# Edge counts of a graph kernel stored as bytes, cast by ScalarE, with other sizes of transfer and another schedule of the matrix writes

## Chip, core and metric

One core of a Trainium2 chip runs the whole program in one launch. The metric is device time in microseconds. The kernel before took 3538.95 us, the median of three runs (3537.87 to 3542.65).

## What is computed

The reference is a block of two graph networks on 6250 nodes of 256 features, with 100000 edges that come sorted by destination. First an attention layer, then three SAGE layers, each on the normalised activations and added to them. Cut to what matters here:

```python
h = relu(layernorm(x))
x = x + attention(h, edge_attr_16, edge_attr_4, ..., src, dst)
h = relu(layernorm(x))
for l in range(3):
    msg = relu(h @ pW[l] + pb[l])[src]
    agg = segment_sum(msg, dst)
    mean = agg / maximum(deg, 1)
    out = mean @ lW[l] + lb[l] + h @ rW[l]
    h = out / norm(out)              # silu after layers 0 and 1
x = x + layernorm(h) * ln_w + ln_b
```

## The kernel before, in words

Nodes are tiled into 49 blocks of 128 (`BLOCKS`), edges into 782 tiles of 128, seven tiles to a chunk of the attention (`CHUNKS` = 112). The program is three phases with a barrier between them: `prepare` (node projections), `attention`, and `layers` (three sweeps, one per SAGE layer). Every engine runs its own list of instructions in order, written out by hand; semaphores order them against each other.

**The two ways in which messages are summed.** For destinations from column 2008 on (`FIRST_TILE` = 251), POOL gathers the message rows of the source nodes by indirect DMA, 128 rows at a time (line 1174, 531 gathers in each sweep), and PE sums them with small one-hot matrices (line 1310). For the first 2048 destinations (`DENSE`) the sum is a dense product instead: a matrix of edge counts, 6272 sources by 2048 destinations, is built in DRAM once (`m.adj`, fp32) and streamed in each sweep. A step of the dense product (`sweep_step`, lines 1233 to 1242) takes one block of 128 sources and 512 destination columns: two fp32 matmuls of 128x128 by 128x512 (line 1240). There are 4 passes by 49 blocks = 196 steps in a sweep. `stream` on SP (lines 1179 to 1186) loads for each step a 128x512 piece of the matrix (line 1184) and the 128x256 message block (line 1186) into one of six buffers (`STREAM`), and waits for PE to free it.

**How the matrix is built, inside the attention phase.** DVE finds for each of the first 261x128 edges how many edges of the same cell stand before and after it (`count_piece`, lines 587 to 612): 18 pieces, one in every second chunk from chunk 2 on (`COUNT_FROM`), then `place_cells` makes the cell's address and count. SP clears the matrix with 49 stores, one per chunk from chunk 1 (`ZERO_FROM`, line 1673). POOL then writes the counts by indirect DMA, 128 cells at a time (`place_edges`, line 580), 261 writes in all: from chunk 60 on (`BUILD_FROM`), evenly over the chunks, with 44 left (`LATE_CELLS`) until after the last chunk's gathers.

**The order in the attention.** POOL gathers the seven tiles of chunk c (line 571) once chunk c - 7 is summed (`RING` = 7 buffers, the wait on `summed`), and in the same list come the matrix writes. The other engines run a pipeline over several chunks: PE projects and transposes scores of later chunks while it sums earlier ones (line 1743, and line 1751, which ends a chunk and releases its buffer). `layers` begins when POOL has seen all its writes land (`built`) and the other engines have drained.

**The order in a sweep.** It has 67 chunks of up to eight edge tiles. In chunk q, PE sums the gathered tiles (line 1310), then does the dense steps that `steps_done(q)` gives, three or four of them, and within them the work on one node block: `combine` (line 1278), `project` (line 1288). ACT in chunk q runs `keep` (line 1472, the gathered sums out of PSUM), then for a node block `first` (lines 1481, 1485) and `second` (square at line 1493, Silu at line 1496), and after each of the four passes `turn` (line 1515, two copies of 128x512). SP in chunk q sends the loads for the steps up to `steps_done(q - 1)` + 6 and then stores finished message blocks (line 1207). POOL gathers up to ten groups of tiles ahead (`QUADS`), and waits for `summed`.

Of the kernel before, what the change touches and what calls it, by code (L numbers as in the profile page):

```python
# [30 lines left out]
int32 = mybir.dt.int32  # L31
ALU = mybir.AluOpType
# [3 lines left out]
P = 128  # L36
N, E, D = 6250, 100000, 256
HEADS, HD, KINDS, FEATS = 8, 32, 4, 16
LAYERS = 3
# [48 lines left out]
COUNT_FROM = 2  # L88
COUNT_ROOT = 32
ZEROS = 1024  # L90
# [7 lines left out]
ZERO_FROM, BUILD_FROM, LATE_CELLS = 1, 60, 44  # L98
# [1038 lines left out]

def layers(nc, m, a):
# [5 lines left out]
                            stream0=None, stream1=None, stream2=None, stream3=None, stream4=None, stream5=None,  # L1144
                            streamed=STREAM, turned=1,
# [18 lines left out]
    with stack:  # L1164
# [13 lines left out]
        def _(sp):  # L1178
            def stream(w, d):

                u = w.step0 + d
                k, j, part = u % STREAM, d % BLOCKS, d // BLOCKS
                sp.wait_ge(s["streamed"].sem, s["streamed"].free(u))
                sp.dma_start(m.a_rows[:, k, 0:PASS_COLS[part]],
                             m.adj[j * P:(j + 1) * P, PASS_AT[part]:PASS_AT[part] + PASS_COLS[part]]).then_inc(s[f"stream{k}"], 16)
                sp.dma_start(m.m_rows[:, k, :], block_rows(m.tables[w.l], j)).then_inc(s[f"stream{k}"], 16)
# [22 lines left out]
            sp.dma_start(m.dst_at, m.at_dram).then_inc(s["places"], 16)  # L1209
            for w in sweeps:  # L1210
# [21 lines left out]
        def _(pe):  # L1232
            def sweep_step(w, d):
                u = w.step0 + d
                k, j, cols = u % STREAM, d % BLOCKS, PASS_COLS[d // BLOCKS]
                pe.wait_ge(s[f"stream{k}"], 32 * (u // STREAM + 1))
                if j == 0:
                    pe.wait_ge(s["turned"].sem, s["turned"].free(w.pass0 + d // BLOCKS))
                for half in range(2):
                    last = nc.tensor.matmul(m.ps[:, 2 + half, 0:cols], m.m_rows[:, k, half * P:(half + 1) * P], m.a_rows[:, k, 0:cols],  # L1240
                                            start=(j == 0), stop=(j == BLOCKS - 1))
# [224 lines left out]
        def _(act):  # L1466
# [50 lines left out]

            for w in sweeps:
                turns = 0

                def chunk(q):
                    nonlocal turns
                    i = w.slot_at(q)
                    if q < WORK - 1:
                        keep(w, q)
# [12 lines left out]
def attention(nc, m, a):  # L1538
# [48 lines left out]
    with stack:  # L1587
        @block.gpsimd
        def _(pool):
            placed = 0  # L1590
            for c in range(CHUNKS):
# [14 lines left out]
        def _(sp):  # L1606
# [56 lines left out]
            for c in range(steps):  # L1663
# [6 lines left out]
                if ZERO_FROM <= c < ZERO_FROM + BLOCKS:  # L1670
                    if c == ZERO_FROM:
                        sp.wait_ge(s["zeros"].sem, 1)
                    sp.dma_start(block_rows(m.adj, c - ZERO_FROM).rearrange("p (k n) -> p k n", n=ZEROS),
                                 m.zero_rows[:, None, :].to_broadcast([P, DENSE // ZEROS, ZEROS])).then_inc(s["zeroed"], 16)
# [754 lines left out]
```

## Time and profile before

| | |
|---|---|
| median of three runs | 3538.95 us |
| span of the profiled execution | 4184.6 us |
| prepare, attention, three sweeps in the profile | 0 to 103, 103 to 1747, 1747 to 4184 us |
| PE busy in the profile | 3193.8 us (76%) |
| POOL busy in the profile | 2554.3 us (61%) |
| DVE, ACT busy | 1555.7 (37%), 1014.1 (24%) |
| mean granted clock of TensorE | 0.821 |
| moved by DMA | 769.06 MB, mean 184 GB/s |

The profiled execution has no time of its own beside its span: 4184.6 us from the first to the last instruction, 18% above the median of the runs. Durations below are that execution's. "Idle before" is the time for which an engine stood still before an instruction, with what ended it; a releaser "remote" or "issue" is one that the profile could not name. In the tables by stretch, the columns are the stretch, its length, the busy time of PE, PEld (weight loads), DVE, ACT and POOL in this order with the number of instructions behind each, the granted clock, the mean busy share of the 16 DMA engines, and GB/s; a table of one line shows only the engine of that line. TensorE's granted clock is a share of 2.4 GHz and takes the two values 1.0 and 0.5; the figures are means.

### The profile page before, as it was taken

How to read it: one execution, taken by the hardware profiler on the slowest of the kernel's cores; microseconds unless marked ns; L12 is line 12 of the kernel's file. 1: busy time of each engine (PE TensorE's matmuls, PEld its weight loads, DVE VectorE, ACT ScalarE, POOL GpSimd, SP SyncE). 2: the span in 40 equal slices, each digit the busy share in tenths (PEclk: the TensorE clock that was granted, in tenths of full speed). 3: DMA queues.
4: the chain of work that ended last, by engine and by line, in shares of the span. 5: the costliest groups of instructions: out<-in, count | busy, mean ns of one | idle time of the engine just before them, and what ended most of it. 6: DMA issues, size and time to landing. Idle time of an engine off the chain costs nothing. (4 is left out here: it accounts for less than half of the span.)

```text
span 4184.6 us, 42792 instructions
## 1 busy us (share of the span) xinstructions
PE 3193.8 (76%) x12377; PEld 1800.4 (43%) x12377; DVE 1555.7 (37%) x5405; ACT 1014.1 (24%) x2500; POOL 2554.3 (61%) x2686
## 2 busy tenths in 40 slices
PE   6488888777676764678889976888989668788874
PEld 4366667555454552324334432343434323333332
DVE  5166766443343441312222322122322312434345
ACT  4255555433343431201111111011111100000000
POOL 2566566666666667266666664666666556666663
PEclk9577778766677775779999987899999878898985
DMA  7588788644444442356666743666766356776762
GB/s 206 157 278 274 258 275 289 172 123 125 120 129 125 129 131 53 111 183 208 205 207 206 222 138 125 198 213 214 215 209 215 98 163 214 221 226 223 222 195 73
DMA packets 472972, 769.06 MB, mean 184 GB/s; under 512 B 118971, under 2 KB 293840, under 8 KB 472736
## 3 DMA queue, kind: packets, MB, share of 16 engines
q1 hardware_dynamic: 348368, 435.20, 32.1%
q0 software_dynamic: 123984, 331.08, 27.6%
q8 instruction: 103, 1.69, 0.2%
q14 instruction: 133, 1.09, 0.1%
q10 hardware_dynamic: 384, 0.00, 0.0%
HBM read 658.09 MB, written 107.88 MB: 183 GB/s over the span
## 5 line engine op out<-in xcount | busy, mean ns | idle before, releaser
L1174 POOL DMA_INDIRECT ring<-message_table,src_index x1593 | 1514.4, 951 | 946.7 <-issue 440.5
L1240 PE MATMUL ps<-ring,attention_work 128*128 128x512 f32 x2352 | 1181.6, 641 | 175.3 <-issue 122.2
L571 POOL DMA_INDIRECT ring<-attention_table,src_index x784 | 757.8, 967 | 488.0 <-issue 211.7
L1240 PEld LDWEIGHTS ps<-ring,attention_work 128*128 128x128 f32 x2352 | 465.4, 204 | 737.5 <-issue 700.8
L1743 PE MATMUL ps<-ring,one_hot 128*128 128x265 f32 x1568 | 624.6, 511 | 154.4 <-issue 152.6
L1743 PEld LDWEIGHTS ps<-ring,one_hot 128*128 128x128 f32 x1568 | 349.0, 246 | 235.8 <-issue 202.6
L1472 ACT ACTIVATE ring<-ps 128x256 f32<-128x256 f32 (+1 forms) x201 | 76.6, 381 | 1265.2 <-DMA attention_work<-run_flags 1141.9
L1704 PEld LDWEIGHTS ps<-attention_work 128*128 128x128 f32 x1568 | 320.3, 248 | 111.7 <-issue 33.2
L1310 PE MATMUL ps<-ring,attention_work 128*32 128x256 f32 x3186 | 304.8, 417 | 54.9 <-issue 54.4
L1387 DVE TENSOR_TENSOR attention_work<-attention_work,ps 128x160 f32<-128x160 f32 (+2 forms) x231 | 65.4, 295 | 725.1 <-DMA root<-in_x 481.0
L1405 DVE SCALAR_TENSOR_TENSOR block_o<-ps,inv_deg,root 128x256 f32<-128x256 f32 x147 | 71.1, 484 | 642.4 <-remote 388.8
L1704 PE MATMUL ps<-attention_work 128*128 128x32 f32 x1568 | 276.5, 299 | 42.8 <-issue 26.1
L580 POOL DMA_INDIRECT dense_adjacency<-times,cell x261 | 256.9, 984 | 79.5 <-issue 79.5
L1278 PE MATMUL ps<-w_l,attention_work 128*128 128x256 f32 x588 | 175.2, 425 | 117.2 <-issue 67.3
L1946 ACT ACTIVATE attention_work<-attention_work,window_p 128x896 f32<-128x896 int32 x112 | 116.2, 1037 | 558.6 <-DMA right_scores<-attention_work 453.4
L1958 ACT ACTIVATE one_hot<-iota_row,dst_rel 128x128 f32<-128x128 f32 x784 | 239.9, 391 | 0.0
L1695 PE MATMUL ps<-attn_edge,attention_work 112*128 112x224 f32 x224 | 77.4, 432 | 204.9 <-DVE attention_work L1810 148.7
L1856 DVE TENSOR_TENSOR ring<-ring,ps 128x1792 f32<-128x1792 f32 x112 | 224.0, 2000 | 23.5 <-issue 13.4
L1288 PE MATMUL ps<-w_pr,block_hT 128*128 128x512 f32 x392 | 203.5, 645 | 26.8 <-issue 16.5
L1252 PE MATMUL ps<-attention_work,ring 128*128 128x144 f32 (+1 forms) x804 | 167.1, 335 | 65.3 <-issue 31.3
L1278 PEld LDWEIGHTS ps<-w_l,attention_work 128*128 128x128 f32 x588 | 119.0, 210 | 198.2 <-issue 129.6
L1252 PEld LDWEIGHTS ps<-attention_work,ring 128*128 128x128 f32 (+1 forms) x804 | 121.1, 207 | 159.6 <-issue 114.8
(183 smaller groups left out, 3058.4 us busy)
## 6 DMA issues: line engine op xcount, KB each, us to landing
ring<-dense_adjacency SPq DMA_DIRECT2D x588, 256.0 KB
attention_work<-message_table SPq DMA_DIRECT2D x588, 128.0 KB
attention_work<-in_dst_edges SPq DMA_DIRECT2D x112, 448.0 KB
dense_adjacency<-root SPq DMA_DIRECT2D x49, 1024.0 KB
ring<-message_table,src_index POOLq DMA_INDIRECT x1593
attention_sums<-sums_out SPq DMA_DIRECT2D x112, 132.5 KB
ring<-attention_table,src_index POOLq DMA_INDIRECT x784
message_table<-attention_work SPq DMA_DIRECT2D x98, 128.0 KB
```

Source lines behind the costliest of these rows:

```text
L571: pool.indirect_dma_start(m.ring[:, k, t, 0:cols], None, table, bass.IndirectOffsetOnAxis(ap=m.src[:, at:at + 1], axis=0)).then_inc(s[f"ro ...
L580: pool.indirect_dma_start(cells, bass.IndirectOffsetOnAxis(ap=m.cell[:, j:j + 1], axis=0), m.times[:, j:j + 1], None, bounds_check=BLOCKS ...
L1174: pool.indirect_dma_start(m.quad_ring[:, k, j, :], None, m.tables[w.l], bass.IndirectOffsetOnAxis(ap=m.src[:, t:t + 1], axis=0)).then_inc( ...
L1240: last = nc.tensor.matmul(m.ps[:, 2 + half, 0:cols], m.m_rows[:, k, half * P:(half + 1) * P], m.a_rows[:, k, 0:cols], start=(j == 0), stop ...
L1252: last = nc.tensor.matmul(m.ps[:, 1, k * VIEW:(k + 1) * VIEW], m.kept_sums[0:rows, u % 2, k * P:(k + 1) * P], m.lane_put[0:rows, u % 2, :] ...
L1278: last = nc.tensor.matmul(m.ps[:, 0, 0:D], sides[k], m.w_l[:, w.l, k, :], start=(k == 0), stop=(k == 1))
L1288: last = nc.tensor.matmul(m.ps[:, 5, :], m.b_hT[:, k * P:(k + 1) * P], m.w_pr[:, w.l + 1, k, :], start=(k == 0), stop=(k == 1))
L1310: last = nc.tensor.matmul(m.ps[j * LANE:(j + 1) * LANE, 6 + u % 2, 0:D], m.lane_hot[:, u % 2, j * DEPTH + r, :], m.quad_ring[:, v % QUADS, ...
L1704: last = nc.tensor.matmul(m.ps[:, 0, t * 32:(t + 1) * 32], m.one_hotT[:, t * P:(t + 1) * P], m.right[:, c % EDGES, :], start=False, stop=F ...
L1743: last = nc.tensor.matmul(m.ps[:, 6 + parity, 0:SUMC], m.one_hot[:, parity, t, :], m.ring[:, k, t, 0:SUMC], start=(t == 0), stop=(c == 0 a ...
L1856: nc.vector.tensor_tensor(ring_heads[k][:, :, :, 0:HD], ring_heads[k][:, :, :, 0:HD], weights[:, :, :, None].to_broadcast([P, TILES, HEADS ...
L1958: last = nc.scalar.activation(m.one_hot[:, c % 2, t, :], m.iota_row[:, 0:P], ACT.Abs, bias=m.dst_rel[:, at:at + 1], scale=-1.0)
```

## The change

The matrix of counts is kept as unsigned bytes in DRAM, and the counts that POOL writes are bytes. In the sweeps, SP loads seven blocks of the matrix in one DMA of bytes (`bunch`, 448 KB, two buffers in the space of `one_hot`), and ACT casts each 128x512 piece to fp32 into the six buffers that PE reads (`cast`, one ACTIVATE Copy per step, 588 in all), at the head of its work in each chunk. Message blocks come two at a time into eight buffers (`pair_runs`: 100 DMAs in a sweep, one for two blocks except where a pass begins inside a pair). PE waits for the pair and for the cast, where it waited for one semaphore of both loads. The clearing is 14 stores of 896 KB instead of 49 of 1024 KB, in chunks 1 to 14. The counting has a piece in each chunk from chunk 1. POOL's matrix writes begin at chunk 27, and 84 are left until after the last gathers.

```diff
-COUNT_FROM = 2
+COUNT_FROM = 1
-ZEROS = 1024
+ZEROS = 896
+ZERO_STORES = 14
+BUNCH = 7
+BUNCHES = 2
+HELD_ROWS = 8
+HELD_PAIRS = HELD_ROWS // 2
-ZERO_FROM, BUILD_FROM, LATE_CELLS = 1, 60, 44
+ZERO_FROM, BUILD_FROM, LATE_CELLS = 1, 27, 84
...
+def pair_runs(x):
+    first, second = 2 * x % STEPS % BLOCKS, (2 * x + 1) % STEPS % BLOCKS
+    return [(0, first, 2)] if second else [(0, first, 1), (1, second, 1)]
...
         def _(sp):
+            def bunch(g):
+                if g >= LAYERS * STEPS // BUNCH:
+                    return
+                if g >= BUNCHES:
+                    sp.wait_ge(s["cast"].sem, s["cast"].done((g - BUNCHES + 1) * BUNCH - 1))
+                d = g * BUNCH % STEPS
+                j, part = d % BLOCKS, d // BLOCKS
+                sp.dma_start(m.a_small[:, g % BUNCHES], ...).then_inc(s[f"small{g % BUNCHES}"], 16)
             def stream(w, d):
                 u = w.step0 + d
-                sp.wait_ge(s["streamed"].sem, s["streamed"].free(u))
-                sp.dma_start(m.a_rows[:, k, 0:PASS_COLS[part]], ...)
-                sp.dma_start(m.m_rows[:, k, :], block_rows(m.tables[w.l], j))...
+                if u % BUNCH == BUNCH // 2:
+                    bunch(u // BUNCH + 1)
+                if u % 2:
+                    return
+                if u >= HELD_ROWS:
+                    sp.wait_ge(s["streamed"].sem, s["streamed"].done(u + 1 - HELD_ROWS))
+                for at, j, rows in pair_runs(u // 2):
+                    sp.dma_start(m.m_rows[:, (u + at) % HELD_ROWS:(u + at) % HELD_ROWS + rows, :], ...)
...
+            bunch(0)
             for w in sweeps:
...
             def sweep_step(w, d):
-                pe.wait_ge(s[f"stream{k}"], 32 * (u // STREAM + 1))
+                pe.wait_ge(s[f"pair{u // 2 % HELD_PAIRS}"], pair_landed(u // 2))
+                pe.wait_ge(s["cast"].sem, s["cast"].done(u))
...
+            def cast(u):
+                g, j = divmod(u, BUNCH)
+                act.wait_ge(s[f"small{g % BUNCHES}"], 16 * (g // BUNCHES + 1))
+                if u >= STREAM:
+                    act.wait_ge(s["streamed"].sem, s["streamed"].done(u - STREAM))
+                nc.scalar.activation(m.a_rows[:, u % STREAM, :], m.a_small[:, g % BUNCHES, j, :], ACT.Copy)...
+            ready = 0
...
                 def chunk(q):
                     i = w.slot_at(q)
+                    while ready < min(w.step0 + (steps_done(q - 1) if q else 0) + STREAM, LAYERS * STEPS):
+                        cast(ready)
+                        ready += 1
                     if q < WORK - 1:
                         keep(w, q)
...
-                        pool.wait_ge(s["zeroed"], 16 * BLOCKS)
+                        pool.wait_ge(s["zeroed"], 16 * ZERO_STORES)
...
-                if ZERO_FROM <= c < ZERO_FROM + BLOCKS:
+                if ZERO_FROM <= c < ZERO_FROM + ZERO_STORES:
...
-                if c >= COUNT_FROM and (c - COUNT_FROM) % 2 == 0:
-                    piece = (c - COUNT_FROM) // 2
+                if c >= COUNT_FROM:
+                    piece = c - COUNT_FROM
...
-    m.adj = dram("dense_adjacency", BLOCKS * P, DENSE)
+    m.adj = nc.dram_tensor("dense_adjacency", (BLOCKS * P, DENSE), uint8, kind="Internal").ap()
-        m.times = sb("times", [P, OWN])
+        m.times = sb("times", [P, OWN], uint8)
```

## Rows read from the trace of the kernel before

**Rows 1.** Windows: stretch, us, busy of each engine, clock, DMA share, GB/s

```profile
207.00:415.00 208.00, 168.90 (x734) 133.81 (x732) 140.63 (x320) 109.18 (x252) 133.10 (x134) 0.80 0.86 277
415.00:655.00 240.00, 205.15 (x874) 161.28 (x874) 169.20 (x422) 130.73 (x306) 142.80 (x147) 0.80 0.83 270
655.00:780.00 125.00, 109.33 (x494) 85.86 (x493) 77.14 (x227) 72.94 (x173) 79.46 (x85) 0.86 0.84 259
780.00:1605.00 825.00, 568.72 (x2062) 415.53 (x2060) 322.59 (x949) 311.00 (x732) 550.08 (x570) 0.70 0.45 126
1605.00:1747.00 142.00, 66.58 (x216) 43.21 (x214) 49.58 (x164) 34.24 (x91) 54.08 (x57) 0.67 0.14 39
```

**Rows 2.** The same stretches, the gathers of line 571 alone

```profile
207.00:415.00 208.00, 133.10 (x134) 0.80 0.86 277
415.00:655.00 240.00, 142.80 (x147) 0.80 0.83 270
655.00:780.00 125.00, 79.46 (x85) 0.86 0.84 259
780.00:1605.00 825.00, 340.85 (x358) 0.70 0.45 126
```

**Rows 3.** The same, the matrix writes of line 580 alone

```profile
780.00:1605.00 825.00, 209.23 (x212) 0.70 0.45 126
1605.00:1747.00 142.00, 47.69 (x49) 0.67 0.14 39
```

**Rows 4.** Lines 580 and 571, POOL: ns least/median/most, first and last start

```profile
L580 POOL DMA_INDIRECT dense_adjacency<-times,cell x261: 966/973/1172, 788.6 to 1674.8; - x131
...
L571 POOL DMA_INDIRECT ring<-attention_table,src_index x784: 940/946/3228, 103.3 to 1612.3; - x196
```

**Rows 5.** Waits of POOL from 780 to 1605 us: total us, times, longest

```profile
POOL ring L571 <- issue: 96.3, 316, 0.3
POOL ring L571 <- remote: 94.6, 37, 3.9
...
POOL ring L571 <- PE ps L1751: 21.3, 5, 4.9
```

**Rows 6.** Timeline of PE, attention, a slow stretch: start, us, what, idle

```profile
1208.64 0.60 PE L1743 MATMUL ps<-ring,one_hot 128*128 128x265 f32 x1 [1.80 <-issue]
1210.74 0.60 PE L1743 MATMUL ps<-ring,one_hot 128*128 128x265 f32 x1 [1.49 <-issue]
```

**Rows 7.** Timeline of POOL at the end of the attention

```profile
1746.99 0.99 POOL L1174 DMA_INDIRECT ring<-message_table,src_index  x1 [71.17 <-POOLq L153]
```

**Rows 8.** Lines 608 and 600, DVE, the counting: busy us, mean ns | idle

```profile
L608 DVE TENSOR_REDUCE root<-root 128x261 f32<-128x2088 f32 x12 | 49.7, 4144 | 0.0
...
L600 DVE TENSOR_TENSOR root<-keys 128x2472 f32<-128x2472 f32 x6 | 16.3, 2720 | 0.0
```

**Rows 9.** Windows of the first and third sweep, columns as in rows 1

```profile
1747.00:2562.00 815.00, 676.55 (x2604) 302.39 (x2604) 211.85 (x930) 110.71 (x321) 503.86 (x531) 0.90 0.61 189
...
3372.00:4184.00 812.00, 608.62 (x2310) 269.66 (x2310) 291.35 (x1216) 57.82 (x124) 507.40 (x531) 0.83 0.63 197
```

**Rows 10.** Timeline of one chunk of the first sweep, PE

```profile
2211.07 0.64 PE L1310 MATMUL ps<-ring,attention_work 128*32 128x256 f32 x8
...
2213.18 3.60 PE L1240 MATMUL ps<-ring,attention_work 128*128 128x512 f32 x8
```

**Rows 11.** The same chunk, ACT

```profile
2210.78 0.51 ACT L1496 ACTIVATE block_h<-block_o,block_inv_norm 128x256 f32<-128x256 f32 x1 [2.01 <-issue]
```

**Rows 12.** Line 1515, ACT, copies of 128x512

```profile
L1515 ACT ACTIVATE attention_work<-ps x24: 576/592/606, 1941.5 to 4060.1; 128x512 f32<-128x512 f32 x24
```

**Rows 13.** Line 1240, PE, the dense product

```profile
L1240 PE MATMUL ps<-ring,attention_work 128*128 128x512 f32 x2352 | 1181.6, 641 | 175.3 <-issue 122.2 <-ACT attention_work L1515 27.1 <-DMA attention_work<-message_table 25.6
```

**Rows 14.** DMA issues on the page: count, KB each

```profile
ring<-dense_adjacency SPq DMA_DIRECT2D x588, 256.0 KB
...
dense_adjacency<-root SPq DMA_DIRECT2D x49, 1024.0 KB
```

More of the change, by code:

```diff
@@ L1135, in ring_pieces, with pair_landed @@
     return pieces
+def pair_runs(x):
+    first, second = 2 * x % STEPS % BLOCKS, (2 * x + 1) % STEPS % BLOCKS
+    return [(0, first, 2)] if second else [(0, first, 1), (1, second, 1)]
+def pair_landed(x):
+    return 16 * sum(len(pair_runs(y)) for y in range(x % HELD_PAIRS, x + 1, HELD_PAIRS))
 def layers(nc, m, a):
@@ L1143, in layers @@
                             consts=0, places=None, onehot=0, summed=2, kept=2, flipped=2, merged=1,
[L1144 to L1145 removed]
+                            small0=None, small1=None, pair0=None, pair1=None, pair2=None, pair3=None,
+                            cast=0, streamed=0, turned=1,
                             lmm=1, o=1, norm2=0, floor=0, newton=0, inv_norm=0, h=1,
@@ L1239, in sweep_step @@
                 for half in range(2):
-                    last = nc.tensor.matmul(m.ps[:, 2 + half, 0:cols], m.m_rows[:, k, half * P:(half + 1) * P], m.a_rows[:, k, 0:cols],
+                    last = nc.tensor.matmul(m.ps[:, 2 + half, 0:cols], m.m_rows[:, u % HELD_ROWS, half * P:(half + 1) * P], m.a_rows[:, k, 0:cols],
                                             start=(j == 0), stop=(j == BLOCKS - 1))
@@ L1516, in turn @@
                 last.then_inc(s["turned"].sem, 1)
+            def cast(u):
[3 more added lines that the diff above has]
+                    act.wait_ge(s["streamed"].sem, s["streamed"].done(u - STREAM))
+                nc.scalar.activation(m.a_rows[:, u % STREAM, :], m.a_small[:, g % BUNCHES, j, :], ACT.Copy).then_inc(s["cast"].sem, 1)
+            ready = 0
             for w in sweeps:
@@ L1521, in chunk @@
                 def chunk(q):
-                    nonlocal turns
+                    nonlocal turns, ready
                     i = w.slot_at(q)
+                    while ready < min(w.step0 + (steps_done(q - 1) if q else 0) + STREAM, LAYERS * STEPS):
+                        cast(ready)
+                        ready += 1
                     if q < WORK - 1:
@@ L1669, in _ @@
                     load(c + EDGES - 1)
-                if ZERO_FROM <= c < ZERO_FROM + BLOCKS:
+                if ZERO_FROM <= c < ZERO_FROM + ZERO_STORES:
                     if c == ZERO_FROM:
                         sp.wait_ge(s["zeros"].sem, 1)
-                    sp.dma_start(block_rows(m.adj, c - ZERO_FROM).rearrange("p (k n) -> p k n", n=ZEROS),
-                                 m.zero_rows[:, None, :].to_broadcast([P, DENSE // ZEROS, ZEROS])).then_inc(s["zeroed"], 16)
+                    pieces = BLOCKS * DENSE // (4 * ZEROS * ZERO_STORES)
+                    first = (c - ZERO_FROM) * pieces * 4 * ZEROS
+                    sp.dma_start(m.adj.rearrange("(p r) d -> p (r d)", p=P)[:, first:first + pieces * 4 * ZEROS].rearrange("p (k n) -> p k n", k=pieces),
+                                 m.zero_rows[:, None, :].to_broadcast([P, pieces, 4 * ZEROS])).then_inc(s["zeroed"], 16)
                 if 1 < c <= CHUNKS + 1:
@@ L2324, in build @@
         at[0] = 0
-        m.m_rows = part(work, STREAM * D).rearrange("p (k e) -> p k e", k=STREAM)
+        m.m_rows = part(work, HELD_ROWS * D).rearrange("p (k e) -> p k e", k=HELD_ROWS)
         m.agg_t = part(work, 2 * HALF).rearrange("p (k e) -> p k e", k=2)
```

20 lines of the change are left out of this document (12 added, 8 removed).

## The prediction

> **What bounds the kernel now.** I read the profile by stretch, since three phases have three limits.
>
> First the attention phase from chunk 8 on [rows 1]. Between 207 and 780 us no engine is full but PE is close: 205 of 240 us, then 109 of 125. From 780 us on, PE falls to 569 of 825 and POOL rises to 550. The gathers alone tell the pace [rows 2]: seven make a chunk, so 147 in 240 us is 11.4 us a chunk, 85 in 125 is 10.3, and 358 in 825 us is 51.1 chunks at 16.1 us. The reader is to see that the jump falls on the chunk where the matrix writes begin: 212 of them stand in that stretch [rows 3], the first at 788.6 us [rows 4].
>
> POOL's own need: a gather takes 0.946 us and a write 0.973 [rows 4], and each is followed by 0.30 us of idle issue (96.3 us in 316 times [rows 5]), so 1.25 and 1.28 us. A chunk without writes needs 7 x 1.25 = 8.8 us of POOL, less than its pace of 10.3 to 11.4: there POOL has spare time. A late chunk has 212 / 51.1 = 4.15 writes and needs 8.8 + 5.3 = 14.1 us. The other 2.0 us of 16.1 are POOL's waits for a free buffer: 94.6 + 21.3 = 116 us in 51 chunks, 2.3 us each [rows 5]. So POOL's writes carry the late chunks, and PE adds stalls, some of them in slow stretches where its matmuls stand 2 us apart [rows 6].
>
> Then the sweeps [rows 9]. A sweep takes 815 us, POOL needs 531 x 1.25 = 664, and PE is busy for 677. Inside a dense chunk PE's work runs on without a hole: sums at 2211.07, dense steps from 2213.18 for 3.6 us [rows 10]. ACT has 111 busy us in a sweep, DMA a share of 0.61. Neither is near a limit.
>
> **The change, part by part,** against the 4184.6 us of the profiled execution.
>
> A. *Writes from chunk 27.* 261 - 84 = 177 writes go over 85 chunks, 2.08 each, 2.7 us. POOL's need is 8.8 + 2.7 = 11.4 us a chunk in all of them. I take the one-byte write at 0.973 us, as the four-byte one: POOL makes 128 addresses either way (the gather of long rows takes 0.946, the slowest write 1.172, so it is bounded from both sides). From chunk 27 (415 us) to chunk 111 (1605 us) there are 84 chunk times in 1190 us. The new chunk time is not in the trace. Its lower end is POOL's 11.4; its upper end is 11.4 plus today's late excess, 2.1, so 13.5. Of the late stretch PE is busy 569 / 51.1 = 11.1 us a chunk, against 109.3 / 12.1 = 9.0 in the stretch from 655, so PE is near POOL's need and some excess stays; I take a little over half of it: 12.6. 84 x 12.6 = 1058: **-132 us** (958 to 1134, so -232 to -56). The 33 chunks up to 780 us become slower (11.1 to 12.6, +50) and the 51 later ones faster (16.1 to 12.6, -180).
>
> What must be ready: POOL's wait at chunk 27 is for the counting and the clearing. Counting now ends at DVE's chunk 19, clearing at SP's chunk 14, and POOL runs at most seven chunks ahead, so DVE is at chunk 20 or later. No wait.
>
> B. *Counting in every chunk, clearing in fewer.* The 18 pieces cost DVE 49.7 + 16.3 = 66 us [rows 8], 3.7 each. DVE is now busy 77.1 / 12.1 = 6.4 us in a chunk without pieces. With one in each of chunks 1 to 19, it has 10.1 and more, about the present pace of 10.9 (134 gathers in 208 us [rows 2]). It may add up to 2 us in 19 chunks, and takes its present half of that from the chunks up to 38, where POOL's need will set the time anyway. **+15 us** (0 to +38). The 35 stores that go carried 38 MB [rows 14]; DMA's share of 0.86 falls, but from 655 us on, still at 0.84, chunks ran at 10.3, so this traffic held back little: nothing.
>
> C. *84 writes at the end.* Today POOL has 49 instances of line 580 after 1605 us [rows 3] and then stands idle for 71.2 us before the barrier [rows 7], in a tail of 142 us. After: 7 gathers and 84 writes, 8.8 + 107 = 116 us, and 2 for landing. The others drain seven chunks in that time; at 12.6 instead of 16.1 us a chunk their 142 us become 117. Both end together at 118: **-24 us** (0 to -24; POOL is the new last, so it can't be more).
>
> D. *The sweeps.* Off goes 192 KB of the 384 KB of each step: the matrix goes from 256 to 64 [rows 14]. On goes a cast per step on ACT, 588 in all. The nearest row is the copy of 128x512, 0.592 us [rows 12]: 116 us a sweep, beside 111 us that ACT has now, in 815. Both lie beside PE. What each new wait could hold up: a cast waits for the step six before it, at the latest the last dense step of the chunk before; behind it on ACT stands `keep`, which waits for sums that PE makes later still. `keep` feeds a product one chunk on. SP's wait for a cast is for one at least four steps back. A bunch is sent some ten microseconds before its first cast. SP issues 84 + 300 DMAs instead of 1176, and its stores of line 1207 stand behind fewer. Where PE starts a sweep it now waits for less; all waits of the dense product on message loads are 25.6 us of 175 idle [rows 13]. I take **-6 us** for three starts (0 to -25), and 0 for the casts; their cost without cover is the second rival.
>
> Sum: -132 + 15 - 24 - 6 = **-147 us** of 4184.6, to 4038.
>
> The measured median is 3538.95, 0.846 of the profiled span, and the profile can't say which stretch is shorter outside it. But not all can be as profiled: 2638 indirect DMAs at 1.25 us are 3298 us, and with 103 us of prepare, the idle 71 and two starts of sweeps that leave little room. So POOL's issue must be quicker unprofiled, and I scale the whole: -124 us, **3415 us**, -3.5%.
>
> **A rule weighed against the trace.** The granted clock is 0.86 where PE is busy 109 of 125 us, 0.70 where it is busy 569 of 825 [rows 1], and 0.90 in the sweep with 677 of 815 [rows 9]: busier stretches have the higher share of 2.4 GHz. The Trainium skill, "TensorE: Matmul & The Clock Gate", section "What's actually happening", says that the gate is closed by default and that recent activity opens it. By that rule the trace agrees, and packing the late chunks would raise the clock by itself, which my sum leaves out.
>
> **Rivals.**
>
> *1. More than that: POOL alone sets the chunk.* If the clock rises as the chunks close up, PE's 11.1 us falls towards the 9.0 of the stretch at 0.86, and PE's stalls with it. Then 84 x 11.4 = 958: -232 + 15 - 24 - 6 = -247, scaled -209: 3330 us. For it: the clock rows. Against: PE's late slow stretches came while POOL was writing, and nothing shows that they go. 20%.
>
> *2. Slower: the casts are exposed.* Place: ACT's order in a sweep. Silu of the chunk ends at 2210.78 + 0.51 = 2211.29 [rows 11], just as PE begins the next sums; then come 3.4 casts, 2.0 us, to 2213.3. PE's first dense steps at 2213.18 use casts of the chunk before, and those behind the combine begin at 2216.8 [rows 10]: 3.5 us of slack. If ACT or the loads run later than that, PE waits in each of 201 chunks. The gain of 147 is gone at 0.73 us a chunk. With two casts exposed, 1.2 us, it is 241 - 147 = +94, scaled +80: 3619 us. The slack speaks against it; that the faster unprofiled run may eat it speaks for it. 12%.
>
> *3. Small gain: PE sets the late chunks.* If the slow stretches [rows 6] stay, chunks run at 13.5: -56 + 15 + 0 - 6 = -47, scaled -40: 3499 us. 16%.
>
> *4. Nothing: the writes only change place.* If PE's stalls make up the 16.1 and the early chunks pay the 50 us of part A, gains and losses cancel within 7 us: 3539 us. Against it: the pace jumped exactly with the first write. 6%.
>
> **How the numbers follow.** Forecast 46%, rival 1 20%, rival 3 16%, rival 4 6%, rival 2 12%. A measurement of this kernel tells about 0.2% (7 us) from no change. Faster 46 + 20 + 16 = 82%, same 6%, slower 12%. The forecast's own spread, with chunk times of 12.1 to 13.1, is 3380 to 3455. The range goes from just below rival 1, 3320, to just above rival 3, 3505; outside lie rivals 2 and 4 and a little beside.
>
> **What would show it.** Right: gathers of chunks 27 to 111 in some 1058 us at an even pace, about 177 writes among them; POOL idle before its first sweep gather for a few microseconds instead of 71.2; sweeps of 805 to 815 us with ACT busy near 225 and DMA's share near 0.45. Wrong in A: a pace of 13.5 or more with POOL's waits for buffers grown. Wrong in B: chunks 1 to 19 over 13 us. Wrong in D: idle time before line 1240 ended by ACT's cast, and sweeps above 830 us. A sweep much under 790 us would mean that the loads held PE back in a way that the rows don't show.

## The result and the profile after

| | before | after |
|---|---|---|
| median | 3540.8 us (3537.87 to 3543.02) | 3514.49 us (3512.33 to 3515.39) |
| ratio, 95% interval | | 0.9922 [0.9909, 0.9934] |
| span of the profiled execution | 4184.6 us | 3512.3 us |
| PE, POOL, ACT busy | 3193.8, 2554.3, 1014.1 | 2879.6, 2563.6, 1352.7 |
| mean granted clock | 0.821 | 0.901 |
| moved by DMA | 769.06 MB | 614.88 MB |

The change saves 26 us, 0.8%. The forecast was 3415 us and its range 3320 to 3505: the sign was right, the size was not, and the time lies outside the range.

The spans cannot be compared as they stand. The profile of before ran for 18% longer than the kernel's median; the profile of after agrees with its median within 0.1%. Profiling by itself therefore adds nothing here. Before was then timed on two chips: on one it takes 4240.7 us (and its profile looks like the one that the prediction read), on the other 3539 to 3543 us. The median that was to be predicted is like the second chip's. So the rows ahead of the prediction describe the wrong machine, and I compare after with a profile of before on the second chip (run c1_before_third, span 3533.2 us, measured 3535.47). Two things are inferred and not shown: which chip gave the profile of 4184.6 us, and that it is the chip and not its condition at that hour that makes the difference, since the slow chip was used in one session only.

Windows of before on that chip, columns as in rows 1; the stretches are chunks 28 to 60, chunk 60 to the last gather, the tail (from there to the first sweep), and the first sweep.

```profile
357.00:672.00 315.00, 277.14 (x1313) 221.80 (x1314) 233.92 (x624) 197.66 (x461) 215.20 (x225) 0.89 0.93 303
672.00:1396.00 724.00, 471.77 (x2124) 372.58 (x2124) 330.76 (x978) 323.57 (x750) 550.67 (x569) 0.80 0.53 146
1396.00:1480.00 84.00, 42.75 (x151) 27.38 (x149) 37.96 (x131) 22.36 (x63) 54.40 (x56) 0.78 0.20 53
1480.00:2163.00 683.00, 627.47 (x2604) 292.22 (x2604) 211.68 (x930) 117.22 (x321) 504.77 (x532) 0.96 0.73 225
```

The same of after. Its writes begin at 357 us, so the first stretch is longer.

```profile
357.00:737.00 380.00, 290.98 (x1380) 231.62 (x1378) 215.80 (x641) 211.90 (x492) 288.96 (x299) 0.88 0.66 183
737.00:1326.00 589.00, 447.51 (x2077) 356.23 (x2078) 320.96 (x949) 313.64 (x727) 448.13 (x463) 0.87 0.63 175
1326.00:1459.00 133.00, 41.90 (x158) 27.64 (x156) 40.30 (x137) 23.35 (x67) 91.67 (x95) 0.69 0.14 34
1459.00:2140.00 681.00, 629.10 (x2604) 293.34 (x2604) 212.49 (x930) 227.88 (x523) 504.47 (x531) 0.97 0.59 170
```

And the matrix writes alone, before (line 580) and after (line 586), where [rows 3] showed 212 and 49.

```profile
672.00:1396.00 724.00, 209.00 (x212) 0.80 0.53 146
1396.00:1480.00 84.00, 47.72 (x49) 0.78 0.20 53
```

```profile
357.00:737.00 380.00, 68.12 (x68) 0.88 0.66 183
737.00:1326.00 589.00, 106.16 (x106) 0.87 0.63 175
1326.00:1459.00 133.00, 84.84 (x88) 0.69 0.14 34
```

POOL's instructions less its writes are its gathers, seven to a chunk. Before: 225 gathers in 315 us are 9.8 us a chunk, then 357 in 724 are 14.2. After: 231 in 380 are 11.5, and 357 in 589 are 11.5 again. The late chunk time fell from 14.2 to 11.5, and 11.4 is what the prediction gave as POOL's own need. But the early stretch pays for it with +65 us (68 writes that it did not have and 6 gathers that before had made by 357 us, less the waits below), the late one gets 135 back, and the tail pays +49 (39 more writes): -21 us in all, the whole difference of the two spans (20.9).

Where the 21 us come from is in POOL's own rows. Busy time and idle before, with releasers, of the attention's gathers and writes, before:

```profile
L571 POOL DMA_INDIRECT ring<-attention_table,src_index x784 | 757.5, 966 | 279.8 <-issue 233.4 <-PE ps L1751 36.7 <-POOLq L153 9.6
L580 POOL DMA_INDIRECT dense_adjacency<-times,cell x261 | 256.7, 984 | 79.5 <-issue 79.5
```

The same rows of after, and POOL's waits from 104 to 1459 us (total us, times, longest us; "issue" is POOL's own 0.30 us behind each instruction):

```profile
L577 POOL DMA_INDIRECT ring<-attention_table,src_index x784 | 764.3, 975 | 248.9 <-issue 238.3 <-POOLq L159 9.7 <-PE ps L1801 1.0
L586 POOL DMA_INDIRECT dense_adjacency<-times,cell x261 | 259.1, 993 | 79.5 <-issue 79.5
```

```profile
POOL ring L577 <- issue: 238.3, 782, 0.3
POOL dense_adjacency L586 <- issue: 79.5, 261, 0.3
POOL ring L577 <- POOLq L159: 9.7, 1, 9.7
POOL ring L577 <- PE ps L1801: 1.0, 1, 1.0
```

In the attention of both kernels POOL is never idle but for the 0.30 us behind each instruction, for 9.6 us once at its start, and for waits on PE for a free buffer. These waits are 36.7 us before, of which 34.3 in nine waits between 357 and 672 us, at a DMA share of 0.93; 1.0 us after. That is -35.7. (The clearing of before ran from 146 to 630 us; up to 357 us POOL waited for PE for 0.3 us only, since it starts up to seven chunks ahead.) Against it the same 1045 instructions are a little longer: gathers +6.8, writes +2.4, issue 312.9 to 317.8, +4.9. Together -21.6.

POOL is also last at the end of the attention, in both (e8_no_late and e5_late0 below test this). The timeline of POOL there, before and then after; [rows 7] showed 71.17 us of idle time in this place:

```profile
1466.25 0.97 POOL L580 DMA_INDIRECT dense_adjacency<-times,cell  x1 [0.30 <-issue]
1480.36 0.99 POOL L1174 DMA_INDIRECT ring<-message_table,src_index  x1 [13.14 <-POOLq L153]
```

```profile
1445.34 0.97 POOL L586 DMA_INDIRECT dense_adjacency<-times,cell  x1 [0.30 <-issue]
1459.38 0.99 POOL L1192 DMA_INDIRECT ring<-message_table,src_index  x1 [13.07 <-POOLq L159]
```

The sweeps take 683 and 681 us. POOL's 531 gathers are busy for 504 us and have 0.30 us of issue each, 159: 664 of them. ACT has its casts, 228 us busy instead of 117, and the DMA share falls from 0.73 to 0.59; neither moves the time.

### The profile page after: what moved, and what is told of

Its sections match the earlier page's. It is cut to its first block and busy times, and to the rows that moved or that the text cites. A ratio compares the mean times of both kernels' runs of the same rounds, so it can differ in the third digit from the quotient of the medians.

```text
span 3512.3 us, 43710 instructions
## 1 busy us (share of the span) xinstructions
PE 2879.6 (82%) x12377; PEld 1673.2 (48%) x12377; DVE 1549.3 (44%) x5405; ACT 1352.7 (39%) x3088; POOL 2563.6 (73%) x2686
## 2 busy tenths in 40 slices
DMA packets 450790, 614.88 MB, mean 175 GB/s; under 512 B 105739, under 2 KB 355872, under 8 KB 450544
## 3 DMA queue, kind: packets, MB, share of 16 engines
q0 software_dynamic: 123984, 330.98, 34.3%
## 5 line engine op out<-in xcount | busy, mean ns | idle before, releaser
L1276 PE MATMUL ps<-ring,attention_work 128*128 128x512 f32 x2352 | 1102.8, 613 | 114.1 <-DMA attention_work<-message_table 93.3
L1793 PE MATMUL ps<-ring,one_hot 128*128 128x265 f32 x1568 | 527.0, 454 | 23.9 <-issue 22.3
L1560 ACT ACTIVATE ring<-one_hot 128x512 f32<-128x512 uint8 x588 | 335.2, 618 | 266.8 <-PE ps L1276 190.1
L1793 PEld LDWEIGHTS ps<-ring,one_hot 128*128 128x128 f32 x1568 | 310.8, 218 | 88.4 <-issue 53.9
L1762 PE MATMUL ps<-ring,ident 128*128 128x224 f32 x224 | 95.2, 517 | 244.2 <-DMA ring<-attention_table,src_index 244.2
L1754 PEld LDWEIGHTS ps<-attention_work 128*128 128x128 f32 x1568 | 254.5, 199 | 33.1 <-ACT attention_work L1999 8.7
L1346 PEld LDWEIGHTS ps<-ring,attention_work 128*32 128x32 f32 x3186 | 65.2, 110 | 352.4 <-issue 164.0
L1860 DVE TENSOR_TENSOR attention_work<-ps,attention_work 128x224 f32<-128x224 f32 x112 | 43.7, 390 | 427.8 <-PE ps L1762 421.0
L1754 PE MATMUL ps<-attention_work 128*128 128x32 f32 x1568 | 220.2, 259 | 7.1 <-ACT attention_work L1999 7.1
L2018 ACT ACTIVATE sums_out<-ps 128x265 f32<-128x265 f32 x112 | 43.8, 391 | 443.1 <-PE ps L1801 439.3
## 6 DMA issues: line engine op xcount, KB each, us to landing
attention_sums<-sums_out SPq DMA_DIRECT2D x112, 132.5 KB, 3.0
```

The source lines that it names most:

```text
L1346: last = nc.tensor.matmul(m.ps[j * LANE:(j + 1) * LANE, 6 + u % 2, 0:D], m.lane_hot[:, u % 2, j * DEPTH + r, :], m.quad_ring[:, v % QUADS, ...
L1560: nc.scalar.activation(m.a_rows[:, u % STREAM, :], m.a_small[:, g % BUNCHES, j, :], ACT.Copy).then_inc(s["cast"].sem, 1)
L1754: last = nc.tensor.matmul(m.ps[:, 0, t * 32:(t + 1) * 32], m.one_hotT[:, t * P:(t + 1) * P], m.right[:, c % EDGES, :], start=False, stop=F ...
L1793: last = nc.tensor.matmul(m.ps[:, 6 + parity, 0:SUMC], m.one_hot[:, parity, t, :], m.ring[:, k, t, 0:SUMC], start=(t == 0), stop=(c == 0 a ...
```

## The experiments

The recorded expectations name their theories by letters. P: POOL's list sets the time of everything, and a write costs the same wherever it stands; its first form gave the whole gain to the schedule of the writes and none to the bytes. B: the lighter DMA traffic of the bytes is what pays; D is its sharper form, that it is the clearing's traffic in the chunks up to 60. S: the gain is in the sweeps' loads or in fewer instructions on SP. X: the casts cost something (in e2 it only marks a time below both others). C: part C of the prediction. T: PE sets the time. Q: the dense counting is free. The first four runs were on the chip of 4240 us, the others on the chip of 3540 us, and each is compared with runs of before on its own chip.

| run | median us | before us | ratio, 95% |
|---|---|---|---|
| e1_old_schedule | 4225.71 | 4240.72 | 0.9971 [0.9949, 0.9992] |
| e2_schedule_alone | 4280.66 | 4240.72 | 1.0097 [1.0066, 1.0127] |
| e3_late44 | 4227.74 | 4240.72 | 0.9967 [0.9948, 0.9986] |
| a1_after_again | 3516.64 | 3539.49 | 0.9939 [0.9922, 0.9955] |
| e1b_old_schedule | 3509.24 | 3539.49 | 0.9919 [0.9903, 0.9936] |
| e2b_schedule_alone | 3592.32 | 3539.49 | 1.0153 [1.0136, 1.017] |
| e3b_late44 | 3513.49 | 3543.22 | 0.9916 [0.9898, 0.9935] |
| e4_old_count | 3512.44 | 3543.22 | 0.9914 [0.99, 0.9927] |
| e6_double_cast | 3516.78 | 3543.22 | 0.9926 [0.9909, 0.9943] |
| e7_extra_clear | 3546.08 | 3543.22 | 1.0011 [1.0001, 1.0021] |
| e8_no_late | 3448.48 | 3540.89 | 0.9741 [0.9719, 0.9762] |
| e5_late0 | 3554.95 | 3540.89 | 1.0044 [1.003, 1.0057] |
| a2_after_third | 3515.96 | 3540.89 | 0.9935 [0.991, 0.996] |

**Before again, on the first chip.** No edit; 4244.66 us in its one execution (it is not in the table).

> The kernel before, profiled once more, because the changed kernel's profile spans 3512.3 us beside a measured 3514.5, while the profile of before spanned 4184.6 beside 3541. Theory P (POOL's issue of indirect DMAs sets the time of both kernels, at 1.25 us a gather also outside a profile, and the earlier profile was one with a disturbed TensorE): span of 3535 to 3545, chunks 60 to 111 at 14.1 to 14.4 us, sweeps of 680 to 690 us, the mean granted clock near 0.90. Theory T (PE sets the late chunks of before, and profiling itself adds time to before): span near 4180 again, late chunks at 16 us, sweeps at 810.

Its page, its late chunks and first sweep (windows, columns as in rows 1), and its waits of POOL in the late chunks:

```profile
span 4242.3 us, 42792 instructions
...
PE 3205.0 (76%) x12377; PEld 1794.1 (42%) x12377; DVE 1557.2 (37%) x5405; ACT 1010.6 (24%) x2500; POOL 2563.8 (60%) x2686
```

```profile
787.00:1621.00 834.00, 585.08 (x2089) 423.60 (x2088) 327.82 (x964) 311.49 (x735) 551.71 (x569) 0.70 0.45 125
1770.00:2593.00 823.00, 676.24 (x2604) 299.64 (x2604) 212.91 (x930) 108.95 (x321) 504.59 (x531) 0.90 0.61 187
```

```profile
POOL ring L571 <- issue: 95.4, 313, 0.3
POOL ring L571 <- remote: 90.7, 36, 4.3
POOL dense_adjacency L580 <- issue: 64.7, 212, 0.3
POOL ring L571 <- PE ps L1751: 33.5, 8, 5.2
```

These are the rows of the prediction within some per cent but for the waits on PE, 33.5 us where it had 21.3 ([rows 1, 5, 9]), and here the timed kernel does take 4240 us. So this regime is not the profiler's. POOL is as fast as on the other (2563.8 busy us against 2555.0 us); PE is not (3205.0 against 2896.1 for the same 12377 matmuls), and stops in places like those of [rows 6].

**The change with the old schedule of the writes**, on both chips. Writes from chunk 60 and 44 late, all else as after:

```diff
-ZERO_FROM, BUILD_FROM, LATE_CELLS = 1, 27, 84
+ZERO_FROM, BUILD_FROM, LATE_CELLS = 1, 60, 44
```

> The changed kernel with only the schedule of the matrix writes put back (from chunk 60, 44 left). Theory P: 3535 to 3545 us, no different from before, since bytes, casts and larger loads lie beside POOL. Theory B (bytes and larger loads also shorten something, by the lighter DMA traffic): 3500 to 3530. Theory X (the casts cost something that the schedule's gain hides): above 3550.

> Bytes, casts and larger loads with the old schedule of the writes, again. On a 3541 chip, theory P: 3535 to 3545; theory B (the lighter traffic is the gain): 3510 to 3525; theory X (casts cost something): above 3550. On a 4240 chip: 4226 as measured, within 20.

On the first chip 4225.71 us, against 4227.74 of e3_late44, whose writes begin at chunk 27: no gain from moving them, there too. On the second 3509.24 against 3516.64 of after, measured beside it: the move costs 7 us, where parts A and C had it save 156 before scaling, 132 after. Theory P in its first form misses too (3535 to 3545): the gain is there without the schedule, as theory B had it. POOL's rows have 5 of them: with the early writes its gathers are busy 2.8 us longer, its writes 1.9 and its issue 3.2, less 3.1 us of waits on PE. This is the fastest of all complete versions, before and after included. Its waits of POOL on PE, and its window, from chunk 28 to chunk 60:

```profile
POOL ring L577 <- PE ps L1801: 0.3, 1, 0.3
```

```profile
361.00:641.00 280.00, 249.17 (x1330) 204.08 (x1329) 205.22 (x606) 201.90 (x471) 212.03 (x224) 0.99 0.82 235
```

224 gathers in 280 us are 8.75 us a chunk: POOL's need of 8.8, with nothing on top. Its whole attention shows 4.1 us of waits on PE, 32.6 less than before, and POOL is 4.0 + 0.5 + 1.7 us longer in gathers, writes and issue: -26.4, where the two medians differ by 30 and the two spans by 28.

**44 writes late instead of 84**, from chunk 27, on both chips.

```diff
-ZERO_FROM, BUILD_FROM, LATE_CELLS = 1, 27, 84
+ZERO_FROM, BUILD_FROM, LATE_CELLS = 1, 27, 44
```

> The changed kernel with 44 writes left until after the last gathers instead of 84. Theory P with a tail set by the other engines' drain: 40 writes at 1.28 us return to the chunks, +51 us, and at most 10 of it comes back in the tail: 3555 to 3566. If instead POOL's 84 late writes set the tail, moving 40 of them costs nothing: 3510 to 3520.

> The changed kernel with 44 writes left until after the last gathers instead of 84, once more, since its first run fell on the chip that takes 4240 us. On a chip that runs before in 3540 us, theory P (POOL is never idle, and is the last engine of the attention phase in either form, so a write costs its 1.28 us wherever it stands): 3510 to 3522, no change from the changed kernel's 3516. Theory C (part C of the prediction: late writes are hidden beside the drain of the others, 40 fewer of them cost 51 us less what the tail gives back): 3530 to 3566. On a 4240 chip: 4228 again, within 15.

3513.49 us, within 0.1% of after: 40 writes moved out of the tail into the chunks change nothing. For the first run theory P still stood with a tail set by the other engines' drain (3555 to 3566), which this refutes; what holds is that POOL's writes set the tail.

**The schedule alone**, on both chips: before, fp32 counts, with the counting in every chunk, writes from chunk 27, 84 late. The 49 clearing stores have to be done by chunk 14, so four go in each chunk.

```diff
-COUNT_FROM = 2
+COUNT_FROM = 1
...
-ZERO_FROM, BUILD_FROM, LATE_CELLS = 1, 60, 44
+ZERO_FROM, BUILD_FROM, LATE_CELLS = 1, 27, 84
...
-                if ZERO_FROM <= c < ZERO_FROM + BLOCKS:
...
+                for b in range(4 * (c - ZERO_FROM), min(4 * (c - ZERO_FROM) + 4, BLOCKS)):
...
-                if c >= COUNT_FROM and (c - COUNT_FROM) % 2 == 0:
-                    piece = (c - COUNT_FROM) // 2
+                if c >= COUNT_FROM:
+                    piece = c - COUNT_FROM
```

> The kernel before with the schedule alone: fp32 matrix, old loads; counting in every chunk, four clearing stores a chunk in chunks 1 to 13, writes from chunk 27, 84 left. Theory P: 3510 to 3525 us, the changed kernel's time, since the gain is POOL's alone. Theory B: 3525 to 3540, as the fp32 clearing (50 MB in 13 chunks) and loads cost what bytes save. Theory X: below 3505.

> The kernel before with the new schedule alone (fp32 matrix, cleared by four stores a chunk in chunks 1 to 13), again. On a 3541 chip, theory P: 3510 to 3525; theory B: 3530 to 3550, because the packed fp32 clearing costs what bytes save. On a 4240 chip: 4281 as measured, within 20.

Slower on both, by 40 and by 53 us, and far above what theory P (3510 to 3525) and theory B (3530 to 3550) expected of the second chip. POOL's waits on PE in chunks 0 to 28:

```profile
POOL ring L571 <- PE ps L1752: 81.0, 9, 16.7
```

All of its waits on PE lie there: 81.0 us against before's 36.7, +44.3; with 8.6 us for longer gathers, writes and issue that is the 53. Packed clearing costs more than spread clearing, and this kernel can't tell the schedule without it. It does suggest that writes as early as these want the byte matrix, whose clearing has a quarter of the bytes to bring out.

**The clearing's traffic put back.** After, with the old schedule, and with 35 stores of 1 MB in chunks 15 to 49 to a tensor that nobody reads. SP and DVE wait for them only late in the phase (not shown in the cut).

```diff
-ZERO_FROM, BUILD_FROM, LATE_CELLS = 1, 27, 84
+ZERO_FROM, BUILD_FROM, LATE_CELLS = 1, 60, 44
...
+                elif ZERO_FROM + ZERO_STORES <= c < 50:
+                    sp.dma_start(m.junk[(c - 15) * P:(c - 14) * P].rearrange("p (k n) -> p k n", n=512),
+                                 m.zero_floats[:, None, 0:512].to_broadcast([P, 4, 512])).then_inc(s["junked"], 16)
```

> Bytes, casts and larger loads with the old schedule of the writes (3509 by itself), and in chunks 15 to 49 a store of 1 MB each into a tensor that nothing reads, so that the attention phase writes as much as the fp32 clearing did. Theory D (the fp32 clearing's traffic made the chunks up to 60 late and POOL wait for buffers, and bytes gained by taking it away): the gain goes, 3528 to 3542, with POOL waits of 20 to 35 us between chunks 28 and 60. Theory S (the gain came from the sweeps' loads or from fewer instructions on SP): 3507 to 3515.

3546.08 us, 37 above e1b, and 0.1% above before: the gain is gone, and a little more than theory D's bounds (3528 to 3542, waits of 20 to 35 us). Its waits of POOL on PE and its window from 365 to 681 us:

```profile
POOL ring L577 <- PE ps L1805: 39.2, 11, 6.9
```

```profile
365.00:681.00 316.00, 279.17 (x1302) 221.67 (x1301) 203.66 (x602) 196.16 (x459) 211.92 (x225) 0.88 0.94 301
```

225 gathers in 316 us, 9.8 us a chunk, a DMA share of 0.94: before's row within a microsecond in length and within four in each busy time but DVE's, whose counting is spread otherwise. This decides for D against S.

The waits show what in a chunk the traffic delays. After every chunk ACT copies the sums out of PSUM into one of two buffers (`sums_out`), from which SP stores them; ACT has to wait until the store of two chunks ago has landed, PE's next chunk waits for ACT's copy, and POOL's buffer waits for PE. ACT's waits before that copy from chunk 28 to 60, in before, in e7 and in e1b, with the time from issue to landing of those stores in e7 and in e1b:

```profile
ACT sums_out L1968 <- DMA attention_sums<-sums_out: 60.6, 22, 5.5
```

```profile
ACT sums_out L2023 <- DMA attention_sums<-sums_out: 70.5, 23, 5.1
DMA to landing us min/median/max: 2.0/5.8/8.9
```

```profile
ACT sums_out L2018 <- PE ps L1801: 60.0, 32, 6.1
DMA to landing us min/median/max: 2.4/3.3/4.4
```

With stores of 1 MB beside it the store of 132.5 KB takes 5.8 us to land and ACT waits for it in 23 of 32 chunks; without them it takes 3.3 us and ACT never waits for it. Loads come late as well: PE's scores wait for a load (`run_flags`) for 13.4 us in before and 18.6 in e7, not at all in e1b, where PE waits for POOL's own gathers instead, 26.8 us. Which of these late DMAs costs how much of the 37 us, no run here separates.

**The counting in every second chunk again**, with the old schedule of the writes: the last thing in which e1b differs from before's attention, beside the clearing and the width of the written cells.

```diff
-COUNT_FROM = 1
+COUNT_FROM = 2
...
-ZERO_FROM, BUILD_FROM, LATE_CELLS = 1, 27, 84
+ZERO_FROM, BUILD_FROM, LATE_CELLS = 1, 60, 44
...
-                if c >= COUNT_FROM:
-                    piece = c - COUNT_FROM
+                if c >= COUNT_FROM and (c - COUNT_FROM) % 2 == 0:
+                    piece = (c - COUNT_FROM) // 2
```

> Bytes, casts and larger loads, with the old schedule of the writes and also the old counting (a piece in every second chunk from chunk 2). The same with counting in each chunk took 3509. Theory P with DVE's counting slowing POOL's own DMA instructions a little: 3500 to 3507. Theory Q (dense counting is free, since POOL is ahead anyway): 3507 to 3512.

A miss of both ranges, by a hair: 3512.44 us, a ratio of 0.9914 against e1b's 0.9919, so no difference that stands out. Gathers until chunk 28 take 993 ns in the mean against 1026 with the dense counting (989 in before), so the counting does lengthen those beside it. But over the whole attention they are busy for 760.4 us against 761.5 in e1b: what the early ones win, the later ones give back, which then have the counting beside them.

**Each cast twice.** A second cast of every piece, into a buffer that nobody reads then, ahead of the real one.

```diff
...
+                if u:
+                    act.wait_ge(s["extra"].sem, s["extra"].done(u - 1))
+                nc.scalar.activation(m.sums_out.rearrange("p k c -> p (k c)")[:, 0:HALF], m.a_small[:, g % BUNCHES, j, :], ACT.Copy).then_inc(s["extra"].sem, 1)
```

> The changed kernel with a second cast of the same piece into an unused buffer before each of the 588, chained by a semaphore: it doubles what ACT was given. Theory P (ACT's casts lie beside POOL's gathers with slack): 3512 to 3522, sweeps of 683 us. Theory X (casts are near exposure, rival 2): 588 x 0.62 = 365 us at most, 3560 to 3880.

3516.78 us, as after. ACT is busy for 323 us in the first sweep and the sweep stays at 682 (windows, columns as in rows 1):

```profile
1454.00:2136.00 682.00, 628.13 (x2604) 291.45 (x2604) 212.02 (x930) 323.31 (x725) 505.22 (x532) 0.97 0.58 170
```

**The late writes taken out, and all of them moved up.** e8_no_late leaves the last 84 writes away, so the counts of those edges are missing from the dense product; e5_late0 sets `LATE_CELLS` to 0 and has all 261 in the chunks.

```diff
-            place_edges(pool, m, s, range(placed, OWN))
-            pool.wait_ge(s["built"], 16 * OWN)
+            pool.wait_ge(s["built"], 16 * (OWN - LATE_CELLS))
```

```diff
-ZERO_FROM, BUILD_FROM, LATE_CELLS = 1, 27, 84
+ZERO_FROM, BUILD_FROM, LATE_CELLS = 1, 27, 0
```

> The changed kernel with its 84 late writes left out, so that the counts of the last 84 x 128 of those edges are missing from the matrix. Theory P (POOL is the last engine of the attention phase, and every write costs its issue): the phase ends earlier by the 84 writes, 107 us, but not before the other engines have drained, which a wait of PE for its first step of the first sweep (75 us long) puts some 75 us before the present start: 3435 to 3450. Theory C (late writes are hidden beside the drain): 3505 to 3516.

> The changed kernel with no write left until after the last gathers. POOL's sum is the same and ends at the same place, but its last gather comes 107 us later, and the other engines must still drain seven chunks behind it. Theory P: the phase now ends with their drain, 45 to 60 us after the last gather, where POOL's end and the barrier took 13: 3545 to 3565. If no difference (3510 to 3520), the drain is shorter than I take it to be.

The end of POOL's attention in e8, then in e5:

```profile
1335.82 0.97 POOL L586 DMA_INDIRECT dense_adjacency<-times,cell  x1 [0.30 <-issue]
1391.69 0.99 POOL L1192 DMA_INDIRECT ring<-message_table,src_index  x1 [54.90 <-POOLq L159]
```

```profile
1438.53 0.97 POOL L586 DMA_INDIRECT dense_adjacency<-times,cell  x1 [0.30 <-issue]
1492.65 0.98 POOL L1192 DMA_INDIRECT ring<-message_table,src_index  x1 [53.15 <-POOLq L159]
```

Without them POOL ends 109.5 us earlier (84 x 1.28 = 107.5), but then stands idle for 54.9 us instead of 13.1, while the other engines drain: -109.5 + 41.8 = -67.7, measured -67.5. With all of them moved up, POOL ends at 1439.5, 7 us earlier than after, and waits for the same drain: the sweeps begin 33 us later, measured +39 (6 us of it I can't place). So the tail can cover 42 us of writes, some 33. The 44 of before are more than that already, so each further one costs its 1.28 us there as in the chunks.

**The references**: before and after once more, on the second chip.

> The kernel before, profiled on whatever chip this job gets. The first job's chip ran it in 4240 us and the measured result came from a chip that ran it in 3541, with matmuls two microseconds apart in the one and not in the other. Theory P (on a chip without those slow stretches POOL's issue sets the time): if the time is near 3541, chunks 60 to 111 at 14.1 to 14.4 us, sweeps of 680 to 690 us, clock near 0.90. Theory T (sweeps bound by PE on both kinds of chip): sweeps of 700 us or more. If the time is near 4240, this chip is of the first kind and the profile repeats the first one within 20 us.

> The changed kernel on the same chip as its companions. On a chip that runs before in 3541 us: 3510 to 3518. On one that runs it in 4240: theory P says that there PE sets the pace, so that the gain comes to 10 to 30 us, 4210 to 4230, as the two partial versions had 4226 and 4228 there.

> The changed kernel as it is, beside the two above. On a chip that runs before in 3540 us: 3512 to 3519. On one that runs it in 4240: theory P leaves PE as the bound there, 4215 to 4235, and then the two others differ from it by less than 40 us.

After took 3514.49, 3516.64 and 3515.96 us in three measurements. Waits of POOL on PE in its attention: 1.0, 1.2 and 1.7 us, where before had 36.7.

## Why the prediction was wrong

*The step that failed first, behind the 3415 us: "So POOL's issue must be quicker unprofiled, and I scale the whole."* An indirect DMA takes 1.25 us in every profile here, on both chips, and the profile of after lasts as long as its timed runs. The sum in that very sentence was the answer: 2638 x 1.25 = 3298 us, with 103 of prepare and some 71 idle, is 3472, just under the 3539 of the median. The median was that of a program in which POOL hardly waits. The profile was of one in which it waits for 266 us in the attention (156.4 for "remote", 78.3 and 31.7 for PE) and for 307 us in the sweeps under one releaser alone. I had the contradiction in hand and explained it away by the one assumption that kept my rows usable. With POOL's list full, 3415 was out of reach: 3298 + 103 and the starts of the three sweeps (13.1, 15.2 and 17.7 us of idle in after) are 3447 already, without the end of the last sweep.

*Part A, -132 us.* The chunk time of "84 x 12.6" fell in the end to 11.5, below my figure: rival 1's mechanism, POOL alone, came true (588 gathers from 357 to 1326 us, 969 us, where rival 1 said 958). What failed is the 16.1 that it was taken from. "the 51 later ones faster (16.1 to 12.6, -180)" was 14.2 to 11.5 on the measured chip, where the 14.2 hold next to no stall (2.1 us of waits on PE from 672 to 1396 us): the gain of 2.7 us a late chunk is the 2.1 writes that left it. In chunks 28 to 60 and the tail they cost the same again. On the first chip, where stalls of PE do stand in the late chunks, moving the writes won nothing either (4227.74 against 4225.71). POOL's waits on PE and on "remote" in its attention were there 278 us in before (run c0, 150.9 + 95.7 + 31.6), 283 with the old schedule and 276 with the writes from chunk 27: they did not shrink. So part A failed on both chips. Rival 4, at 6%, had this outcome in its name ("the writes only change place"), but with another reason: PE's stalls, where it is POOL's full list.

*Part B, +15 us, and "this traffic held back little: nothing".* This is the term that the measured gain belongs to: what stood in the sum as nothing is the whole gain, -35.7 us of waits for buffers, which e7 brings back. I had judged it by a stretch that ran at 10.3 us a chunk at a DMA share of 0.84 [rows 1, 2]. On that profile the reading even holds: the last clearing store stands at 726 us, and the gathers before and behind it, 49 in 71 us and 36 in 54, are 10.1 and 10.5 us a chunk. It says nothing of a chip on which PE does not stall. The comparison to make was with POOL's need of 8.8: at 10.3 to 11.4 us a chunk it waited for 1.5 to 2.6 us in each, before any write, and a suspect for that was what else ran there and nowhere later. The +15 of the dense counting did not show: 1 us of busy time between e1b and e4. (Its 66 us of DVE also leave out ten additions of line 611, 4.4 us.)

*Part C, -24 us.* "Both end together at 118": on the measured chip POOL was the last engine already in before (13.14 us of idle from the last write to the first gather, as long as in after, not 71), so the 40 further late writes cost 51 us there and free 51 in the chunks.

*Part D, -6 us and 0 for the casts.* Right in the main, though the sweeps that it read (815 us) were the other chip's. The sweeps went from 683 to 681, and the double cast shows the slack on ACT: rival 2 had no ground. The cast's row of after:

```profile
L1560 ACT ACTIVATE ring<-one_hot 128x512 f32<-128x512 uint8 x588 | 335.2, 618 | 266.8 <-PE ps L1276 190.1
```

618 ns against the 592 of the nearest row [rows 12]. The Trainium skill, "ScalarE: Activation LUTs", section "What ACT_TABLE_LOAD costs", gives an ACTIVATE with immediates as 186 ns and 0.833 ns for each element of a row, 613 ns for 512. It speaks of fp32 and bf16; this trace agrees for bytes too. The loads of the matrix came down from 154 MB to 38, the DMA share of the sweep to 0.59 (I had said 0.45), and no time came of it: 531 gathers of 1.25 us, 664, fill a sweep of 681. The one-byte write costs what the four-byte one did: 257.2 us for 261 in e1b, 256.7 in before.

*The rule on the clock.* In the late chunks the granted clock rose from 0.80 to 0.87, as PE's busy time went from 472 us of 724 to 448 of 589. By the rule that I cited (the Trainium skill, "TensorE: Matmul & The Clock Gate", section "What's actually happening"), that recent activity opens the gate, the trace agrees again. The clock bought nothing, because PE was not the bound. The mean busy share does not tell the clock by itself: from chunk 28 to 60 before shows 0.89 with PE busy for 277 of 315 us, and e1b 0.99 with 249 of 280.

*The scale.* All in all, the terms A to D measured -21 us between the two spans and -26 between the medians, against -147 before scaling and -124 after it.

*What stays open.* Why PE stands still in stretches on the first chip, and whether it is the chip; why the two versions measured there win 0.3% although POOL's waits in the attention stay (the change itself was not run there); how the 37 us of the clearing traffic divide among the stores and loads that it makes late; and which part of the early writes makes POOL's instructions longer.

## What to carry to other kernels

Lay the profiled span beside the timed median before reading a row; where they differ by more than a per cent, the rows may not be of the machine whose time is to be predicted, and a bound that holds in both (here 2638 indirect DMAs of 1.25 us each) tells more than any stretch. When one engine's in-order list fills the program, moving its instructions is zero-sum, as here: only what makes it wait, or makes its list shorter, changes the time. Look for that in the stretches where its pace is slower than its own need, and ask what runs beside it there, background stores with no deadline among them, and which small store or load of a two-buffer chain they make late.

## What was not expected of the hardware

Two chips ran the same kernel in 3540 and 4240 us, the slower one in one session only. POOL's instructions last the same on both (2555.0 and 2563.8 busy us). The products of line 1743 have medians of 387 and 411 ns, and PE's idle time before them, with no releaser that the profile names, is 29.8 us on one and 147.0 on the other:

```profile
L1743 PE MATMUL ps<-ring,one_hot 128*128 128x265 f32 x1568 | 535.6, 459 | 30.9 <-issue 29.8
```

```profile
L1743 PE MATMUL ps<-ring,one_hot 128*128 128x265 f32 x1568 | 625.5, 511 | 148.3 <-issue 147.0
```

After with the old schedule wins 0.81% on one chip and 0.29% on the other. And 35 clearing stores of 1 MB, which nothing waits for in the chunks, cost 37 us at a DMA share of 0.94, while as many bytes of loads in each sweep (116 MB in three), at 0.73, cost none that can be seen: the sweeps take 683 us with them and 681 without.
